# Adding two sums on GpSimd before TensorE turns them, one step later, in a deformable convolution hidden under attention

## The chip, the cores and the metric

One NeuronCore of a Trainium2 chip. The time is the device time of one execution in microseconds (us), the median of the runs shown.

## The reference

A map of 2 images x 128 channels x 48 x 48 passes four residual layers, each `x = x + layer(groupnorm(x))`, in float32: a deformable depthwise convolution, an involution-like layer, a modulated deformable 3x3 convolution and eight-head attention over the 2304 positions of each image. The change concerns the third layer, whose second image is computed while the attention of the first runs:

```python
sampled = bilinear_gather(x, py, px)        # four weighted corners for each of 9 taps
sampled = sampled * mask[:, None]
out = einsum('bckhw,ock->bohw', sampled, w_dc) + b_dc
```

A sample is the sum of four corners, each with its weight. The weights (bilinear times mask) are ready before this stage.

## The kernel before

The attention stage works through 216 windows. In a window TensorE (PE) does eight pairs: `by_query` (L1817), a product whose row maximum VectorE (DVE) takes (L1671), and `score` (L1801), whose exponential ScalarE (ACT) takes (L1547). Scores go through a ring of three PSUM banks, freed by `exp`; `by_query` and everything that DVE takes go through a ring of four banks, freed by DVE. Between pair 2 and pair 3 of a window PE also does `weigh` (L1839), 32 records that add the previous window's exponentials times the values, and, in four of nine windows, `rows` (L1824), which needs the maxima that GpSimd (POOL) has split into three bf16 parts (`split_max`, L1444 to L1447).

Under this runs the gather of the third layer's second image, 18 tiles of 128 positions. A tile has five steps q = 0 to 4 (called beats in the code), one to a window; the first ten steps lie in a lead of 90 maxima ahead of window 0. All four corners of nine taps lie in `corner[:, j % 2]`, two buffers deep, 9 x 512 numbers for each partition.

- POOL starts the indirect DMAs (`fetch`, L1405), three taps (a group) at a time, into the buffer of tile j + 2 while tile j is being turned. A fetch waits until PE has turned that group of tile j.
- ACT multiplies corners 0 and 3 by their weights (`scale_corner`, L1518), 18 short instructions to a tile, at steps 0 to 4 of the tile before.
- POOL multiplies corners 1 and 2 (`weigh_second`, which first waits for the tile's three groups to land, and `weigh_corner`, both L1393), adds corner 2 to corner 1 and, after ACT is done (`add_first`), corner 3 to corner 0 (L1398). So two half-sums are left, in places 0 and 1.
- PE transposes both half-sums of each tap into the same place of PSUM, where the second is added to the first (`turn_samples`, L1887), one group at each of steps 1, 2 and 3; DVE copies a group to SBUF (`take_turned`, L1699). At step 0 of the next tile PE multiplies the nine taps by `w_dc` (`combine`, L1897), and DVE adds the result to x (L1712). At step 1 it takes statistics (L1717).

The class `Entries` writes down the order in which PE fills the banks, so that each engine knows its counts. Work at a step comes after score 5 of the window on PE and after maximum 5 on DVE.

Of the kernel before, what the change touches and what calls it, by code (L numbers as in the profile page):

```python
# [39 lines left out]
TILES = S // 128  # L40
# [4 lines left out]
GROUPS = 3  # L45
GK = K2 // GROUPS
# [69 lines left out]
def semaphores(ctx, nc, prefix, names):  # L116

    return {n: ctx.enter_context(nc.semaphore(f"{prefix}_{n}")) for n in names.split()}
# [421 lines left out]
def middle_layer(nc, g):  # L540

    with ExitStack() as ctx:
# [63 lines left out]
        with nc.Block() as block:  # L606
# [171 lines left out]
            def _(dve):  # L778
# [208 lines left out]
                for step in range(STEPS):  # L987
                    for j in range(K7):
                        if step < ALL_ROWS:
                            multiply(step, j)  # L990
                        beside(step, j)
# [188 lines left out]
class Entries:  # L1180
# [39 lines left out]

    def beside(self, beat):
        j, q = turned_at(beat)
        if 0 <= j < TILES and 1 <= q <= GROUPS:
            self.ab["turned", j, q - 1] = len(self.ab)
        if q == 0 and 1 <= j <= TILES:
            self.ab["combined", j - 1] = len(self.ab)

# [5 lines left out]
def turned_at(beat):  # L1233
    return divmod(beat - FIRST_BEAT, BEATS)
# [12 lines left out]
def attention_layer(nc, g, out):  # L1247
# [6 lines left out]
    with ExitStack() as ctx:  # L1254
        def sb(name, shape, dt=F32):
            return ctx.enter_context(nc.sbuf_tensor(f"l3_{name}", shape, dt))

        s = semaphores(ctx, nc, "l3", ATT_SEMS)
        ps = g["ps"]
# [18 lines left out]
        turned = sb("turned", [128, K2 * 128])  # L1278
        corner, landed = g["corner2"], g["landed2"]
# [34 lines left out]
        def ab_bank(n):  # L1314
            return AB + n % AB_RING
# [12 lines left out]
        with nc.Block() as block:  # L1328
# [59 lines left out]
            def _(pool):  # L1388
                chain = Chain(pool, s["pchain"])
                def weigh_corner(j, c):  # L1390

                    part_c = corner[:, j % 2, :, c * 128:(c + 1) * 128]
                    chain.link(nc.gpsimd.tensor_tensor(  # L1393
                        part_c, part_c, weight[:, j, :, c].unsqueeze(2).to_broadcast([128, K2, 128]), ALU.mult))

                def add_corner(j, c, d):
                    to, by = (corner[:, j % 2, :, i * 128:(i + 1) * 128] for i in (c, d))
                    return nc.gpsimd.tensor_tensor(to, to, by, ALU.add)  # L1398

                def fetch(j, gr):  # L1400
                    if j >= 2:
                        pool.wait_ge(s["ab_full"], no.ab["turned", j - 2, gr] + 1)
                    for k in range(gr * GK, (gr + 1) * GK):
                        at = (TILES + j) * K2 + k
                        nc.gpsimd.indirect_dma_start(  # L1405
                            corner[:, j % 2, k, :], None, g["table2"],
                            bass.IndirectOffsetOnAxis(ap=g["idx2"][:, at:at + 1], axis=0),
                        ).then_inc(landed[j % 2][gr], 16)
# [15 lines left out]
                def weigh_second(j):  # L1424

                    for gr in range(GROUPS):
                        pool.wait_ge(landed[j % 2][gr], 16 * GK * (j // 2 + 1))
                    weigh_corner(j, 1)

                def add_first(j):  # L1430

                    pool.wait_ge(s["scaled"], j + 1)
                    add_corner(j, 0, 3).then_inc(s["mixed"], 1)

                def take_v(n):
                    nc.gpsimd.tensor_copy(v_s[:, n % 2, :, 0:HD], v_all[:, n, :, :]).then_inc(s["v_slot"], 1)
# [20 lines left out]
                def beat(at):  # L1457
                    j, q = turned_at(at)
                    if q == 0 and 0 <= j < TILES:
                        add_first(j)  # L1460
                    if 0 <= j + 1 < TILES:
                        if q == 1:
                            weigh_second(j + 1)
                        if 2 <= q and j + 2 < TILES:
                            fetch(j + 2, q - 2)
                        if q == 3:
                            weigh_corner(j + 1, 2)
                        if q == 4:
                            chain.link(add_corner(j + 1, 1, 2))

                for n in range(LEAD):
                    if n % 9 == 0:
                        beat(n // 9)
                    if n % WPC == WPC - 1:
                        split_max(n // WPC)
# [145 lines left out]
            def _(dve):  # L1621
                chain = Chain(dve, s["gchain"])
# [73 lines left out]
                def take_turned(j, gr):  # L1696
                    at = no.ab["turned", j, gr]
                    dve.wait_ge(s["ab_full"], at + 1)
                    nc.vector.tensor_copy(turned[:, gr * CH:(gr + 1) * CH], ps[:, ab_bank(at), 0:CH]) \  # L1699
                        .then_inc(s["ab_free"], 1)  # L1700
# [7 lines left out]
                def add_sample(j):  # L1708
                    at = no.ab["combined", j]
                    dve.wait_ge(s["ab_full"], at + 1)  # L1710
                    xt = g["x"][:, (TILES + j) * 128:(TILES + j + 1) * 128]
                    nc.vector.scalar_tensor_tensor(xt, ps[:, ab_bank(at), 0:128], g["b_dc"][:, 0:1], xt,  # L1712
                                                   ALU.add, ALU.add).then_inc(s["ab_free"], 1)

                def sample_stats(j):
                    dve.wait_ge(s["ab_free"], no.ab["combined", j] + 1)
                    ins = nc.vector.bn_stats(g["bst"][:, 1, j, :], g["x"][:, (TILES + j) * 128:(TILES + j + 1) * 128])  # L1717
                    if j == TILES - 1:
                        chain.link(ins)

                def beat(at):
                    j, q = turned_at(at)
                    if 0 <= j < TILES and 1 <= q <= GROUPS:
                        take_turned(j, q - 1)
                    if 1 <= j <= TILES:
                        if q == 0:
                            add_sample(j - 1)
                        if q == 1:
                            sample_stats(j - 1)

                for n in range(LEAD):
                    reduce(n)
                    if n % 9 == 8:
                        beat(n // 9)
# [32 lines left out]
            def _(pe):  # L1767
# [6 lines left out]
                for n in range(HALF):  # L1774
                    side, r = 1 - n // NCH, n % NCH
                    if n >= 3:
                        pe.wait_ge(s["part2"], n - 2)
                    nc.tensor.matmul(ps[:, n % 3, 0:CH], g["wqk"][:, side, :], xg[:, r * CH:(r + 1) * CH],
                                     start=True, stop=True).then_inc(s["proj"], 1)
# [7 lines left out]
                def enter_ab(at):  # L1787
                    if at >= AB_RING:
                        pe.wait_ge(s["ab_free"], at - AB_RING + 1)
                    return ab_bank(at)  # L1790
# [90 lines left out]
                def turn_samples(j, gr):  # L1881

                    pe.wait_ge(s["mixed"], j + 1)
                    bank = enter_ab(no.ab["turned", j, gr])
                    for k in range(GK):
                        for c in range(2):
                            last = nc.tensor.matmul(ps[:, bank, k * 128:(k + 1) * 128],  # L1887
                                                    corner[:, j % 2, gr * GK + k, c * 128:(c + 1) * 128], g["ident"][:, :],
                                                    start=(k == 0 and c == 0), stop=(k == GK - 1 and c == 1),
                                                    is_transpose=True)  # L1890
                    last.then_inc(s["ab_full"], 1)

                def combine(j):
                    pe.wait_ge(s["ab_free"], no.ab["turned", j, GROUPS - 1] + 1)
                    bank = enter_ab(no.ab["combined", j])
                    for k in range(K2):
                        last = nc.tensor.matmul(ps[:, bank, 0:128], g["w_dc"][:, k, :], turned[:, k * 128:(k + 1) * 128],  # L1897
                                                start=(k == 0), stop=(k == K2 - 1))
                    last.then_inc(s["ab_full"], 1)

                def beat(at):
                    j, q = turned_at(at)
                    if 0 <= j < TILES and 1 <= q <= GROUPS:
                        turn_samples(j, q - 1)
                    if q == 0 and 1 <= j <= TILES:
                        combine(j - 1)

# [11 lines left out]
                for w in range(WINDOWS):  # L1919
# [3 lines left out]
                    for j in range(PAIRS):  # L1923
# [12 lines left out]
                        if j == BESIDE:  # L1936
                            beat(WARM + w)
                            if w == NORM_AT + 1:
                                bank = enter_ab(no.ab["means"])
# [153 lines left out]
```

## Time and profile before

| | us |
|---|---|
| median of 3 runs | 2173.13 (2167.44 to 2173.97) |
| span of the profiled execution | 2306.6 |
| gather under the attention, windows 1 to about 84 | 1202 to 1696 |
| attention after the gather | to the end |

The profiled execution took 133 us more than the median run. Durations below are its own. A PE record's end is modelled, and matmuls overlap in the array, so the time that a run of matmuls takes is read from one start to the next.

### The profile page before, as it was taken

How to read it: one execution, taken by the hardware profiler on the slowest of the kernel's cores; microseconds unless marked ns; L12 is line 12 of the kernel's file. 1: busy time of each engine (PE TensorE's matmuls, PEld its weight loads, DVE VectorE, ACT ScalarE, POOL GpSimd, SP SyncE). 2: the span in 40 equal slices, each digit the busy share in tenths (PEclk: the TensorE clock that was granted, in tenths of full speed). 3: DMA queues.
4: the chain of work that ended last, by engine and by line, in shares of the span. 5: the costliest groups of instructions: out<-in, count | busy, mean ns of one | idle time of the engine just before them, and what ended most of it. 6: DMA issues, size and time to landing. Idle time of an engine off the chain costs nothing.

```text
span 2306.6 us, 35479 instructions
## 1 busy us (share of the span) xinstructions
PE 1729.9 (75%) x11841; PEld 913.7 (40%) x11841; DVE 1749.1 (76%) x4137; ACT 1186.2 (51%) x3185; POOL 1097.1 (48%) x1232
## 2 busy tenths in 40 slices
PE   4011112116998988786689999999999999999998
PEld 2011111113554456564434444444444444444443
DVE  5477778777999786784587767777788888888881
ACT  3222222210000145556447877787777777777777
POOL 4676777652666355566386766676513000000000
PEclk8555555556999978998779999999999999999999
DMA  8565566540000144446243332333202101020101
GB/s 266 180 186 176 178 184 188 171 135 5 1 1 1 47 135 145 125 151 217 75 124 92 107 90 88 103 104 96 59 10 35 22 19 30 15 34 14 27 1 42
DMA packets 90855, 212.15 MB, mean 92 GB/s; under 512 B 18512, under 2 KB 43824, under 8 KB 90544
## 3 DMA queue, kind: packets, MB, share of 16 engines
q0 software_dynamic: 51840, 169.91, 24.1%
q1 hardware_dynamic: 38832, 39.97, 7.7%
q8 instruction: 94, 1.54, 0.3%
q14 instruction: 89, 0.73, 0.1%
HBM read 175.21 MB, written 13.37 MB: 82 GB/s over the span
## 4 chain that ended last, share of the span: by engine, by line
PE 43%; ACT 3%; DVE 2%; issue 2%; POOL 1%; another core or an unknown queue 0%; SPq 0%; DMA 0%; ACTq 0%; POOLq 0%
PE ps L1801 13%; PE ps L1839 13%; PE ps L1817 11%; ACT l_e L1547 2%; PE ps L1897 2%; DVE l_mx L1671 1%; PE ps L1824 1%; PE ps L1887 1%; ACT corner L1518 1%; PE ps L1851 1%; PE ps L1857 0%; POOL l_part L1414 0%; POOL corner L1405 0%; PE ps L1878 0%
## 5 line engine op out<-in xcount | busy, mean ns | idle before, releaser
L1671 DVE TENSOR_REDUCE l_mx<-ps 128x1 f32<-128x384 f32 x1728 | 837.5, 550 | 162.7 <-PE ps L1817 145.2
L1547 ACT ACTIVATE l_e<-ps 128x384 f32<-128x384 f32 x1728 | 727.0, 511 | 250.0 <-PE ps L1801 236.4
L1817 PE MATMUL ps<-l_ka,l_qs 96*128 96x384 bf16 x1728 | 574.4, 334 | 16.7 <-DMA l_qs<-l_part 8.7
L1801 PE MATMUL ps<-l_qs,l_ks 99*128 99x384 bf16 x1728 | 565.9, 332 | 23.9 <-ACT l_e L1547 18.3
L810 DVE SCALAR_TENSOR_TENSOR m_prod<-ps,c_b,pad 128x384 f32<-128x384 f32 x588 | 325.3, 611 | 77.1 <-PE ps L1015 59.4
L529 PE MATMUL ps<-c_ident,l_samp 128*128 128x128 f32 x324 | 78.5, 427 | 406.2 <-DVE l_samp L392 314.3
L1839 PE MATMUL ps<-l_e,l_v_s 128*32 128x384 f32 x3456 | 336.1, 495 | 2.0 <-ACT l_e L1547 1.0
L1801 PEld LDWEIGHTS ps<-l_qs,l_ks 99*128 99x128 bf16 x1728 | 165.7, 97 | 397.1 <-ACT l_e L1547 216.1
L1444 POOL CAST l_nsp<-l_nm 128x3 bf16<-128x3 f32 x96 | 18.3, 191 | 545.0 <-DVE l_nm L1676 495.2
L250 POOL DMA_INDIRECT corner<-table,idx x216 | 223.1, 1033 | 105.2 <-issue 62.3
L1015 PE MATMUL ps<-red,c_w 32*128 32x384 f32 x1176 | 200.6, 584 | 50.0 <-DVE m_prod L810 40.4
L626 POOL DMA_INDIRECT corner<-table,idx x162 | 170.3, 1051 | 131.2 <-PE ps L1102 60.2
L529 PEld LDWEIGHTS ps<-c_ident,l_samp 128*128 128x128 f32 x324 | 64.2, 224 | 421.8 <-DVE l_samp L392 325.0
L383 DVE SCALAR_TENSOR_TENSOR l_samp<-corner,wts,l_samp 128x128 f32<-128x128 f32 x648 | 185.2, 347 | 53.0 <-remote 30.1
L1817 PEld LDWEIGHTS ps<-l_ka,l_qs 96*128 96x128 bf16 x1728 | 170.1, 98 | 97.6 <-DVE l_mx L1671 32.5
L1405 POOL DMA_INDIRECT corner<-table,idx x162 | 156.3, 965 | 107.2 <-PE ps L1817 42.7
L614 POOL TENSOR_TENSOR m_prod<-m_prod 128x1152 f32<-128x1152 f32 x55 | 144.7, 2631 | 116.5 <-DVE m_prod L810 116.4
L321 ACT ACTIVATE l_samp<-corner,wts 128x128 f32<-128x128 f32 x216 | 70.4, 391 | 203.2 <-DMA corner<-table,idx 158.6
L1839 PEld LDWEIGHTS ps<-l_e,l_v_s 128*32 128x32 f32 x3456 | 111.8, 109 | 104.5 <-issue 71.3
L1030 PE MATMUL ps<-c_ident,m_prod 128*128 128x128 f32 x1008 | 152.9, 301 | 0.3 <-DVE x_map L825 0.3
L1030 PEld LDWEIGHTS ps<-c_ident,m_prod 128*128 128x128 f32 x1008 | 124.5, 155 | 63.4 <-issue 59.0
L383 DVE SCALAR_TENSOR_TENSOR l_samp<-l_corner,wts,l_samp 128x128 f32<-128x128 f32 x324 | 92.5, 348 | 74.4 <-remote 60.1
(212 smaller groups left out, 1961.0 us busy)
## 6 DMA issues: line engine op xcount, KB each, us to landing
corner<-table,idx POOLq DMA_INDIRECT x540
l_ka<-l_part SPq DMA_DIRECT2D x96, 72.0 KB
l_ks<-l_part SPq DMA_DIRECT2D x96, 72.0 KB
table<-l_tok SPq DMA_DIRECT2D x8, 640.0 KB, 6.4
table<-red SPq DMA_DIRECT2D x8, 640.0 KB, 4.9
l_qs<-l_part SPq DMA_DIRECT2D x90, 48.0 KB
l_qs<-l_part SPq DMA_DIRECT2D x96, 24.0 KB
out<-x_map SPq DMA_DIRECT2D x12, 192.0 KB, 1.9
```

The costliest lines, as they stand in the source:

```text
L250: nc.gpsimd.indirect_dma_start(corners[slot][:, k, :], None, from_row[b], bass.IndirectOffsetOnAxis(ap=idx[:, i * K2 + k:i * K2 + k + 1], ...
L383: last = nc.vector.scalar_tensor_tensor(samp[:, slot, k, :], corners[slot][:, k, j * 128:(j + 1) * 128], wts[:, w:w + 1], samp[:, slot, k, ...
L626: nc.gpsimd.indirect_dma_start(corner[:, i % 2, k, :], None, from_row[0], bass.IndirectOffsetOnAxis(ap=idx[:, i * K2 + k:i * K2 + k + 1], ...
L810: nc.vector.scalar_tensor_tensor(prod[:, slot, j, :].rearrange("p (r w) -> p r w", w=W), ps[:, tap % W_RING, 0:CH].rearrange("p (r w) -> p ...
L1015: last = nc.tensor.matmul(ps[:, tap % W_RING, 0:CH], g["w2"][RED * j:RED * (j + 1), ky, half, :], red_of(c)[RED * j:RED * (j + 1), :], sta ...
L1030: last = nc.tensor.matmul(ps[:, ACC, i * 128:(i + 1) * 128], prod[:, row % RING7, j, i * 128:(i + 1) * 128], g["ident"][:, :], start=(ky = ...
L1405: nc.gpsimd.indirect_dma_start(corner[:, j % 2, k, :], None, g["table2"], bass.IndirectOffsetOnAxis(ap=g["idx2"][:, at:at + 1], axis=0),). ...
L1547: nc.scalar.activation(e[:, w % 2, i, :], ps[:, st_bank(at), 0:QC], ACT.Exp).then_inc(s["st_free"], 1)
L1671: nc.vector.tensor_reduce(mx[:, ga % MAX_SLOTS, u // NQC, u % NQC:u % NQC + 1], ps[:, ab_bank(at), 0:CH], AX.X, ALU.max) \
L1801: nc.tensor.matmul(ps[:, bank, 0:QC], ks[:, head % 2, kt * 128:(kt + 1) * 128], qs[:, gb % 3, j * QC:(j + 1) * QC], start=True, stop=True) \
L1817: nc.tensor.matmul(ps[:, bank, 0:CH], qs[0:KROWS, ga // CT % 3, q0:q0 + 128], ka[:, head % 2, k0:k0 + CH], start=True, stop=True).then_inc ...
L1839: last = nc.tensor.matmul(ps[32 * i:32 * i + 32, AV, 0:QC], v_s[:, (gb * CT + i) // NQC % 2, 2 * at + h, :], e[:, w % 2, h * CT + i, :], s ...
```

## The change

POOL adds the two half-sums as well, so one full sum is left in place 0, and PE turns only this one: nine transposes for a tile and not eighteen. PE turns at steps 2, 3 and 4 and not 1, 2 and 3; DVE's copies and the ring's order move with it. POOL's own steps are laid out anew: both multiplications at step 2, the first addition at step 3, two groups fetched at steps 3 and 4, and the third at step 1 of the next tile.

```diff
     def beside(self, beat):
         j, q = turned_at(beat)
-        if 0 <= j < TILES and 1 <= q <= GROUPS:
-            self.ab["turned", j, q - 1] = len(self.ab)
+        if 0 <= j < TILES and 2 <= q:
+            self.ab["turned", j, q - 2] = len(self.ab)
...
                     pool.wait_ge(s["scaled"], j + 1)
-                    add_corner(j, 0, 3).then_inc(s["mixed"], 1)
+                    chain.link(add_corner(j, 0, 3))
+                    add_corner(j, 0, 1).then_inc(s["mixed"], 1)
...
-                        if q == 1:
+                        if q == 1 and j + 1 > 0:
+                            fetch(j + 1, 2)
+                        if q == 2:
                             weigh_second(j + 1)
-                        if 2 <= q and j + 2 < TILES:
-                            fetch(j + 2, q - 2)
+                            weigh_corner(j + 1, 2)
+                        if 3 <= q and j + 2 < TILES:
+                            fetch(j + 2, q - 3)
                         if q == 3:
-                            weigh_corner(j + 1, 2)
-                        if q == 4:
                             chain.link(add_corner(j + 1, 1, 2))
...
-                    if 0 <= j < TILES and 1 <= q <= GROUPS:
-                        take_turned(j, q - 1)
+                    if 0 <= j < TILES and 2 <= q:
+                        take_turned(j, q - 2)
...
                     for k in range(GK):
-                        for c in range(2):
-                            last = nc.tensor.matmul(ps[:, bank, k * 128:(k + 1) * 128],
-                                                    corner[:, j % 2, gr * GK + k, c * 128:(c + 1) * 128], g["ident"][:, :],
-                                                    start=(k == 0 and c == 0), stop=(k == GK - 1 and c == 1),
-                                                    is_transpose=True)
+                        last = nc.tensor.transpose(ps[:, bank, k * 128:(k + 1) * 128],
+                                                   corner[:, j % 2, gr * GK + k, 0:128], g["ident"][:, :])
...
-                    if 0 <= j < TILES and 1 <= q <= GROUPS:
-                        turn_samples(j, q - 1)
+                    if 0 <= j < TILES and 2 <= q:
+                        turn_samples(j, q - 2)
```

## Rows read from the trace of the kernel before

**Rows 1.** The page's first row: the span.

```profile
span 2306.6 us, 35479 instructions
```

**Rows 2.** Busy time by stretch: with the gather, and after it.

```profile
core 0: us, PE busy (x) PEld busy (x) DVE busy (x) ACT busy (x) POOL busy (x), PEclk, DMA share, GB/s
1202.00:1696.00 494.00, 466.33 (x3474) 236.15 (x3466) 371.82 (x822) 374.63 (x1012) 313.24 (x358) 0.98 0.32 89
1820.00:2200.00 380.00, 380.00 (x2864) 157.47 (x2862) 335.04 (x738) 291.11 (x729) 32.06 (x158) 1.00 0.14 24
```

**Rows 3.** TensorE in time, 1636 to 1692: start, length; tiles 16 and 17.

```profile
1636.71 1.50 PE L1839 MATMUL ps<-l_e,l_v_s 128*32 128x384 f32 x16
...
1643.20 0.52 PE L1839 MATMUL ps<-l_e,l_v_s 128*32 128x384 f32 x3
...
1648.43 1.50 PE L1839 MATMUL ps<-l_e,l_v_s 128*32 128x384 f32 x16
...
1650.70 0.82 PE L1887 MATMUL ps<-c_ident,corner 128*128 128x128 f32 x6
1651.36 0.33 PE L1817 MATMUL ps<-l_ka,l_qs 96*128 96x384 bf16 x1
...
1653.65 0.52 PE L1839 MATMUL ps<-l_e,l_v_s 128*32 128x384 f32 x3
...
1658.69 1.50 PE L1839 MATMUL ps<-l_e,l_v_s 128*32 128x384 f32 x16
...
1663.33 0.52 PE L1839 MATMUL ps<-l_e,l_v_s 128*32 128x384 f32 x3
...
1680.41 1.50 PE L1839 MATMUL ps<-l_e,l_v_s 128*32 128x384 f32 x16
...
1685.34 1.50 PE L1839 MATMUL ps<-l_e,l_v_s 128*32 128x384 f32 x16
...
1689.71 0.52 PE L1839 MATMUL ps<-l_e,l_v_s 128*32 128x384 f32 x3
```

**Rows 4.** Groups by line, 1202 to 1696: busy us, mean ns, idle before and releasers.

```profile
L1671 DVE TENSOR_REDUCE l_mx<-ps 128x1 f32<-128x384 f32 x681 | 332.8, 550 | 90.1 <-PE ps L1817 75.7 <-remote 8.1 <-PE ps L1887 5.6
...
L1405 POOL DMA_INDIRECT corner<-table,idx x135 | 129.6, 960 | 74.2 <-PE ps L1817 42.7 <-issue 25.0 <-PE ps L1801 3.7
...
L1398 POOL TENSOR_TENSOR corner<-corner 128x1152 f32<-128x1152 f32 x33 | 86.8, 2631 | 2.6 <-ACT corner L1518 1.6
...
L1887 PE MATMUL ps<-c_ident,corner 128*128 128x128 f32 x306 | 41.8, 272 | 0.0
...
L1444 POOL CAST l_nsp<-l_nm 128x3 bf16<-128x3 f32 x38 | 7.3, 191 | 86.7 <-issue 47.1 <-DVE l_nm L1676 37.0 <-POOL corner L1393 1.4
```

**Rows 5.** The same view, 1820 to 2200, VectorE's maxima.

```profile
L1671 DVE TENSOR_REDUCE l_mx<-ps 128x1 f32<-128x384 f32 x680 | 326.2, 550 | 43.3 <-PE ps L1817 43.3
```

**Rows 6.** All engines in time: two gathers, then ScalarE and VectorE idle.

```profile
1442.44 0.95 POOL L1405 DMA_INDIRECT corner<-table,idx  x1 [0.30 <-issue]
...
1444.26 0.49 ACT L1547 ACTIVATE l_e<-ps 128x384 f32<-128x384 f32 x1 [1.62 <-PE ps L1801]
...
1444.30 1.02 DVE L1671 TENSOR_REDUCE l_mx<-ps 128x1 f32<-128x384 f32 x2 [1.60 <-PE ps L1817]
```

**Rows 7.** TensorE in time around 1355, where six gathers follow one another.

```profile
1354.86 1.50 PE L1839 MATMUL ps<-l_e,l_v_s 128*32 128x384 f32 x16
...
1361.39 0.34 PE L1801 MATMUL ps<-l_qs,l_ks 99*128 99x384 bf16 x1 [3.29 <-ACT l_e L1547]
...
1365.74 2.79 PE L1839 MATMUL ps<-l_e,l_v_s 128*32 128x384 f32 x16
```

**Rows 8.** Busy time by stretch as in rows 2; DMA traffic behind one group.

```profile
1441.00:1443.00 2.00, 2.00 (x22) 0.92 (x22) 1.70 (x4) 1.62 (x5) 1.50 (x2) 1.00 0.50 154
1443.00:1445.00 2.00, 1.80 (x14) 1.23 (x12) 0.70 (x2) 0.74 (x3) 0.39 (x1) 1.00 0.65 225
```

**Rows 9.** TensorE in time, the first transposes of tile 0.

```profile
1177.88 1.54 PE L1887 MATMUL ps<-c_ident,corner 128*128 128x128 f32 x6 [0.78 <-POOL corner L1398]
```

## The prediction

> **What bounds the kernel now.** I began with the span [rows 1] and cut out the two stretches of the attention that matter: with the gather under it, and after it. After the gather PE is busy for all of its 380 us; with the gather it is busy for 466 of 494 us, at a mean granted clock of 0.98, and POOL for 313 [rows 2]. PE's records overlap, so this says "PE or something near it" and no more. The length of a window says what really ends last, and the view for that is PE in time, read from one `weigh` (L1839) to the next, in a place where no gather runs: tiles 16 and 17 [rows 3]. Tile 16 still has ACT's multiplications (of tile 17), all transposes and no fetch. Its steps take 6.49 us (q = 0, with `combine`), 5.23 (q = 1), 5.22 (q = 2), 5.04 (q = 3) and 4.64 (q = 4, no transposes, two multiplications on ACT and not four). Tile 17 has no multiplications: 4.93 for q = 3 with its transposes, 4.37 for q = 4 with neither.
>
> What these tell: two of ACT's multiplications lengthen a window that has no transposes from 4.37 to 4.64, by 0.27. So ACT, which must free the score banks, sets that window and not PE. Six transposes lengthen a window without multiplications from 4.37 to 4.93, by 0.56; so there PE counts nearly in full. With both, 5.04 to 5.23. Several engines are therefore within 0.3 us of each other in each window, and only `combine`'s window is clearly PE's.
>
> A clean tile takes 6.49 + 5.23 + 5.22 + 5.04 + 4.64 = 26.6 us. In the whole stretch 494 us hold 17 combines, 29.1 us a tile. The other 2.4 us come with the fetches and with each batch's turned sums: rows 6 show what a group's third indirect DMA is followed by, ACT and DVE both idle for 1.6 us until signals of PE come, although PE's own records go on. Where six indirect DMAs follow one another and their data is late, a window lasts from 1354.86 to 1365.74 and the next `weigh` needs 2.79 us and not 1.50 [rows 7].
>
> **Removed from PE.** Nine transposes for each of 18 tiles, 162. Their mean duration is 272 ns [rows 4], but they are pipelined: six run from 1650.70 to the next product's start at 1651.36 [rows 3], 0.11 us each. So at most 162 x 0.11 = 17.8 us, if PE ended every window that has them.
> The Trainium skill (TensorE: Matmul & The Clock Gate, section PE-mode transpose) gives some 275 ns for a transpose in a kernel's context, of bf16, which agrees with this duration. Multiplied out it would make 162 x 0.275 = 44.6 us, an estimate that the starts contradict; I take the starts.
>
> **What of this reaches the windows**, step by step, each with its two ends:
> - q = 0: `combine` as before, 6.49. Change 0.
> - q = 1 loses all six transposes and DVE's copy, and keeps four multiplications and the statistics. By the 4.64 of two multiplications plus 0.27 for two more: 4.91, so -0.32. Ends: -0.59 (as 4.64), 0 (if DVE's statistics and maxima hold it).
> - q = 2: three transposes and not six. PE's part falls by 0.33, ACT's bound of 4.91 remains below it, DVE's copy stays: 5.22 to about 5.05, -0.17. Ends -0.33 and 0.
> - q = 3: 5.04 to about 4.95, -0.09. Ends -0.33 and 0.
> - q = 4 had none and gets three, and DVE's copy: PE's plain 4.37 plus 0.33 is 4.70, above ACT's 4.64; I take +0.13. Ends 0 and +0.33 (it adds in full).
> Sum -0.45 us a tile, x 18 = -8.1 us. All gains and no loss would be the -17.8 above; all losses and no gain +6.
>
> **The first tile.** PE waits 0.78 us for POOL's last addition [rows 9]. Its turn is now a step later, past 9 more maxima (over 4 us), while POOL has one addition more (2.63) and three indirect DMAs fewer before it. The wait goes: -1 us with what DVE idles behind it. Ends 0 and -1.2.
>
> **Added to POOL.** One addition of 2.63 us [rows 4], and a wait for the first one's own result, which no row prices; its work is below POOL's slack that follows, and I take nothing for it. POOL's waits in the stretch: 86.7 us before L1444, 74.2 less the 25.0 of fixed issue gaps before L1405 and 2.6 before L1398 [rows 4], together 139, over 17 tiles 8.1 us. The addition leaves 5.4. Then comes a new wait: `weigh_second` now follows directly on the third group's fetch and waits for it to land. A group is 3 x 128 x 2 KB, 786 KB; 308 KB moved from 1441 to 1443 and 450 KB from 1443 to 1445 [rows 8], while the third issue ended at 1443.39 [rows 6]: so it lands some 2 us after the issue. 3.4 us a tile are left, 2.9 after the tile's own gain. Queued behind that wait on POOL are the two multiplications, 4.3 us, and `split_max`, for which PE's `rows` waits, and behind it all scores. `split_max` runs about two windows ahead of `rows` (its batch's maxima are complete by then), 10 us, so a POOL late by 6.5 us does not reach PE. The full sum is needed at q = 2 and begun at q = 0: two windows for 5.3 us. The cover is POOL's remaining 10%; without it, each us that POOL lacks is a us of each tile, 18 in all.
>
> **The moved fetches.** Still 162 indirect DMAs, none more. Group 0 goes from q = 2 to 3, group 1 from 3 to 4, always behind PE's turning of that group; group 2 from q = 4 to 1 of the next tile, where the condition is long met. ACT needs group 0 at q = 0 (before: over two windows after the earliest start, now over one), group 2 at q = 3, two steps after its fetch: with issues 0.95 + 0.30 us apart [rows 6] and 2 us to landing a group takes 5.5 us, one window, so both are met, group 0 with half a window to spare. SP's loads of keys and queries go by their own waits and are not moved past anything. Groups 0 and 1 can no longer follow back to back, since an addition lies between; rows 7 show what a bad pair costs, 5.7 us over a window of 5.2. Whether this, or new coincidences, weighs more I can't read off: 0, ends -12 (two such windows gone) and +6 (one more).
>
> **DVE.** Nothing is added; its copies move from the step with the statistics to the one with little else. Its maxima take 550 ns with the gather and 550 without [rows 4, 5], so POOL's work beside it does not slow it, and one addition more won't either.
>
> **The sum:** -8.1 - 1.0 = -9.1 us. Against the profiled execution: 2306.6 - 9.1 = 2297.5. The runs' median is 2173.1, 133 us less, and I can't place these 133 us; if the pauses of rows 6 belong to them the steps of rows 3, which have none, hold all the more. I take the difference over one to one: 2164.0.
>
> **Rivals.**
> - PE bounds every window (0.13): the whole 17.8 us, and perhaps a bad pair gone; 2155, down to 2148. For it: PE at 100% after the gather. Against it: 4.64 against 4.37 in rows 3.
> - The change does nothing (0.17): DVE and ACT hold q = 1 to 3 and q = 4 takes back what is won; 2170 to 2176. For it: 5.23 and 5.04 differ by less than PE's 0.66.
> - POOL becomes the bound, the other sign (0.15): its tile is 20.9 of work and issue gaps now (29.1 - 8.1), 23.6 with the addition, 25.6 with the landing wait. In the profiled tile of 28.6 that fits; in a clean one of 26.2 it decides once more than 0.6 us of POOL's waits for PE and for maxima can't be used. With 1.5 us a tile is 27.1, 0.5 over today's 26.6, and 18 tiles make 2182; with 2 us 2191. Place: `weigh_second` at q = 2, then PE idle before L1824 or ACT before L1518.
> - The clock (0.03): PE idles more in ACT's windows and its granted clock falls from 2.4 to 1.2 GHz more often than the 0.98 of rows 2 shows; each case costs `weigh` 2.79 - 1.50 and some products, about 3 us; three more make 2173. The skill's same section has it that transposes do not count as busy for the clock; by it taking them away can't lower the clock, which no row here can show.
>
> **How the numbers follow.** My forecast has 0.52, its own range 2157 to 2170. The measurement tells some 0.3%, 6.5 us: faster is below 2166.6. Of my 0.52 about 0.37 lies there, with 0.13 of the first rival 0.50; slower is the third rival and some coincidences of fetches, 0.17; the rest, 0.33, is within 0.3%. The range leaves a tenth on either side: 2152 (between full gain and forecast) to 2181 (POOL short by about 1.5 us a tile).
>
> **What would show it.** L1887 with 162 records; q = 1 windows near 4.9 and q = 4 near 4.8 where no fetch runs; L1398 with 54 records; POOL idle before L1393 some 2 us each tile, waiting for a DMA, and its other waits near half of 139 us; no idle of PE at the first transposes; `combine`'s windows unchanged. Wrong it would be if PE waited before L1824 for POOL, if ACT idled before L1518 for a DMA, or if windows with a fetch grew: a gather's pause now falls in q = 1, which had none.

## The result, and the profile after

The changed kernel takes 2196.49 us (median of 4 runs, 2193.89 to 2198.81) against 2173.55 of the kernel before: ratio 1.0115, 95% interval 1.009 to 1.014. It is slower by 1.2%, where 2164.0 was forecast and 2181 was the upper end.

First, the page: the span, the shares of the chain of work that ended last, and the groups of GpSimd's (POOL's) fetches and of ACT's multiplications (out and in, count, busy us, mean ns of one, idle before and releaser).

```profile
span 2192.7 us, 35162 instructions
...
PE 35%; POOL 9%; ACT 3%; issue 2%; DMA 2%; DVE 1%; SPq 0%; POOLq 0%; ACTq 0%
...
L1405 POOL DMA_INDIRECT corner<-table,idx x162 | 156.3, 965 | 66.4 <-issue 33.8
...
L1520 ACT ACTIVATE corner<-corner,wts 128x128 f32<-128x128 f32 x324 | 131.0, 410 | 38.7 <-DMA corner<-table,idx 38.5
```

Two more groups, from the view by lines of the whole changed kernel, show that the edit did what it should: 54 additions and 162 transposes.

```profile
L1398 POOL TENSOR_TENSOR corner<-corner 128x1152 f32<-128x1152 f32 x54 | 142.1, 2631 | 2.0
...
L1888 PE MATMUL ps<-c_ident,corner 128*128 128x128 f32 x162 | 27.9, 282 | 0.2
```

ACT is idle for 38.5 us until gathered data lands. Lines of this kernel have moved: `score` is L1803, `weigh` L1841, `rows` L1826.

The span is 114 us under that of [rows 1], although the kernel is slower. So the first profile was not of an ordinary execution. A second profile of the kernel before (label b1_before_again) settles it: its span is 2167.4 and its run 2169.3 us. All comparisons below are against this second profile. In it ACT waits once for this gather's data, 4.2 us, and POOL has 1% of the chain that ended last, against 9% in the changed kernel:

```profile
PE 44%; ACT 4%; DVE 2%; issue 2%; POOL 1%; DMA 0%; SPq 0%; ACTq 0%; POOLq 0%
```

Who waited for whom, both kernels, eleven whole tiles of each: us in total, times, longest. PEld is PE's loading of weights. First the kernel before (second profile), 1147 to 1443:

```profile
POOL corner L1405 <- PE ps L1817: 26.5, 21, 3.6
POOL corner L1405 <- issue: 17.8, 60, 0.3
POOL l_nsp L1444 <- issue: 10.4, 3, 5.4
POOL l_nsp L1444 <- DVE l_nm L1676: 8.9, 4, 2.9
```

The changed kernel, 1155 to 1467:

```profile
POOL corner L1393 <- DMA corner<-table,idx: 28.2, 11, 3.5
POOL corner L1405 <- issue: 20.6, 70, 0.3
ACT corner L1520 <- DMA corner<-table,idx: 19.1, 13, 3.8
PEld ps L1826 <- POOL l_nsp L1448: 11.6, 9, 3.1
PE ps L1826 <- POOL l_nsp L1448: 7.5, 4, 2.9
```

Before, POOL waited for PE and for maxima, and neither PE nor ACT for POOL. After, POOL's waits for others are gone. What is left is one wait a tile for a landing, 28.2 / 11 = 2.6 us, and now PE waits for POOL's `split_max` and ACT for data that POOL fetched late. One case in order of time, on POOL and PE of the changed kernel:

```profile
1286.48 4.33 POOL L1393 TENSOR_TENSOR corner<-corner,wts 128x1152 f32<-128x1152 f32 x2 [1.81 <-DMA corner<-table,idx]
...
1293.66 0.95 POOL L1405 DMA_INDIRECT corner<-table,idx  x1 [0.31 <-issue]
...
1294.62 2.62 POOL L1398 TENSOR_TENSOR corner<-corner 128x1152 f32<-128x1152 f32 x1
...
1298.37 0.22 PE L1826 MATMUL ps<-l_identb,l_nsp 128*3 128x128 bf16 x1 [2.87 <-POOL l_nsp L1448]
```

POOL waits for the landing, multiplies, fetches, adds, and only then reaches `split_max`. DVE had finished these maxima at 1288.7, over eight microseconds before `split_max` began; PE stands for 2.87 us before `rows`, and every score is queued behind it. Two other stalls of PE, of 2.1 us (at 1215.0) and 1.9 us (at 1413.2), go by way of ACT: it stands for 3.8 and 2.8 us before a multiplication until fetched data lands, and PE waits for a score bank.

One more thing follows such a wait. TensorE's granted clock (PEclk, the third number from the end) is full before it and half, 1.2 GHz, for a stretch behind it:

```profile
1290.00:1299.00 9.00, 6.13 (x50) 2.88 (x53) 6.19 (x14) 6.05 (x17) 7.67 (x10) 1.00 0.31 89
1299.30:1302.70 3.40, 3.40 (x18) 1.61 (x10) 1.11 (x2) 1.62 (x5) 2.77 (x4) 0.51 0.54 158
```

Between its first `weigh` and its last `combine` the changed kernel has three such stretches of 3.4 us (from 1121.9, 1299.3 and 1490.5), each within a microsecond of PE's return from a wait of 1.6 to 2.9 us for POOL. The second profile of the kernel before has none between these two points.

### The profile page after: what moved, and what is told of

Its sections match the earlier page's. It is cut to its first block, busy times and chain, and to the rows that moved or that the text cites. A ratio compares the mean times of both kernels' runs of the same rounds, so it can differ in the third digit from the quotient of the medians.

```text
span 2192.7 us, 35162 instructions
## 1 busy us (share of the span) xinstructions
PE 1685.3 (77%) x11679; PEld 875.8 (40%) x11679; DVE 1748.9 (80%) x4137; ACT 1188.7 (54%) x3185; POOL 1156.6 (53%) x1250
## 4 chain that ended last, share of the span: by engine, by line
PE 35%; POOL 9%; ACT 3%; issue 2%; DMA 2%; DVE 1%; SPq 0%; POOLq 0%; ACTq 0%
PE ps L1841 11%; PE ps L1803 11%; PE ps L1819 9%; POOL corner L1405 3%; POOL corner L1398 3%; DMA corner<-table,idx 2%; ACT l_e L1549 2%; POOL corner L1393 2%; PE ps L1896 1%; PE ps L1826 1%; DVE l_mx L1673 1%; ACT corner L1520 1%; PE ps L1859 0%; PE ps L1853 0%; POOL l_part L1414 0%
## 5 line engine op out<-in xcount | busy, mean ns | idle before, releaser
L1803 PE MATMUL ps<-l_qs,l_ks 99*128 99x384 bf16 x1728 | 566.2, 332 | 17.4 <-ACT l_e L1549 12.1
L1841 PE MATMUL ps<-l_e,l_v_s 128*32 128x384 f32 x3456 | 336.1, 495 | 2.4 <-issue 1.2
L1803 PEld LDWEIGHTS ps<-l_qs,l_ks 99*128 99x128 bf16 x1728 | 166.0, 97 | 399.1 <-ACT l_e L1549 227.6
L250 POOL DMA_INDIRECT corner<-table,idx x216 | 230.4, 1067 | 92.3 <-issue 65.5
L1015 PE MATMUL ps<-red,c_w 32*128 32x384 f32 x1176 | 194.2, 573 | 38.7 <-DVE m_prod L810 34.3
L626 POOL DMA_INDIRECT corner<-table,idx x162 | 174.7, 1079 | 74.9 <-issue 46.6
L1405 POOL DMA_INDIRECT corner<-table,idx x162 | 156.3, 965 | 66.4 <-issue 33.8
L1841 PEld LDWEIGHTS ps<-l_e,l_v_s 128*32 128x32 f32 x3456 | 112.3, 109 | 104.2 <-issue 74.4
L1520 ACT ACTIVATE corner<-corner,wts 128x128 f32<-128x128 f32 x324 | 131.0, 410 | 38.7 <-DMA corner<-table,idx 38.5
L723 ACT ACTIVATE corner<-corner,wts 128x128 f32<-128x128 f32 x441 | 136.8, 392 | 23.1 <-DMA corner<-table,idx 23.1
L1030 PE MATMUL ps<-c_ident,m_prod 128*128 128x128 f32 x1008 | 147.4, 293 | 1.3 <-DVE m_prod L819 0.9
```

The lines of the kernel that those rows point to most:

```text
L250: nc.gpsimd.indirect_dma_start(corners[slot][:, k, :], None, from_row[b], bass.IndirectOffsetOnAxis(ap=idx[:, i * K2 + k:i * K2 + k + 1], ...
L626: nc.gpsimd.indirect_dma_start(corner[:, i % 2, k, :], None, from_row[0], bass.IndirectOffsetOnAxis(ap=idx[:, i * K2 + k:i * K2 + k + 1], ...
L1015: last = nc.tensor.matmul(ps[:, tap % W_RING, 0:CH], g["w2"][RED * j:RED * (j + 1), ky, half, :], red_of(c)[RED * j:RED * (j + 1), :], sta ...
L1405: nc.gpsimd.indirect_dma_start(corner[:, j % 2, k, :], None, g["table2"], bass.IndirectOffsetOnAxis(ap=g["idx2"][:, at:at + 1], axis=0),). ...
L1520: ins = nc.scalar.activation(at, at, ACT.Copy, scale=weight[:, j, k, c:c + 1])
L1803: nc.tensor.matmul(ps[:, bank, 0:QC], ks[:, head % 2, kt * 128:(kt + 1) * 128], qs[:, gb % 3, j * QC:(j + 1) * QC], start=True, stop=True) \
```

## Where each step's time went

I read each step from one `weigh` to the next, as in [rows 3], for 16 tiles, from the first `combine` in the windows to the last. Medians in us by q, the mean tile, and the time from the first `weigh` to the kernel's end, which leaves out differences of the earlier layers:

| kernel | q=0 | 1 | 2 | 3 | 4 | mean tile | to the end |
|---|---|---|---|---|---|---|---|
| before, second profile | 6.46 | 5.21 | 5.18 | 5.10 | 4.64 | 26.85 | 1067.6 |
| changed | 6.50 | 4.99 | 5.18 | 5.18 | 4.85 | 27.94 | 1088.8 |
| E1, third group at step 0 | 6.46 | 4.99 | 5.18 | 5.11 | 4.72 | 26.79 | 1065.9 |
| E2, new steps, old sums | 6.46 | 4.99 | 5.19 | 5.11 | 4.94 | 27.05 | 1071.2 |
| E3, nine turned, old steps | 6.46 | 5.18 | 5.19 | 5.11 | 4.64 | 26.71 | 1064.8 |
| E8, ACT's multiplications out | 6.21 | 4.68 | 4.72 | 4.77 | 4.72 | 26.07 | 1054.1 |
| E9, as E8, turned twice | 6.21 | 4.54 | 4.94 | 4.99 | 4.94 | 26.14 | 1054.6 |

The changed kernel's medians are nearly those of before. Its mean is 1.1 us higher because in nine of the sixteen tiles one or two windows of steps 3, 4 and 0 last 0.5 to 3.0 us longer than the same windows before, the longest 9.3 us: 16 x 1.09 = 17.4 us, and 4.3 more lie ahead of these tiles, of 21.2 in all. This is what an engine would look like that falls a little behind in each tile: nothing for some windows, then a stall that pays the debt. The three stretches at half clock are part of the stalls; each can have cost at most half of its 3.4 us, so together at most some 5 of the 21 us (an estimate).

## The experiments

**E1: the third group's fetch at step 0**, ahead of the two last additions.

```diff
+                    if q == 0 and 0 <= j < TILES - 1:
+                        fetch(j + 1, 2)
                     if q == 0 and 0 <= j < TILES:
                         add_first(j)
...
-                        if q == 1 and j + 1 > 0:
-                            fetch(j + 1, 2)
```

> The changed kernel, with the third group's fetch at step 0 ahead of the two last additions and not at step 1. Theory A (GpSimd has become the bound, and 2.6 us of each tile are its new wait for the third group to land): that wait lies under 5.3 us of additions, GpSimd's tile falls from 27.9 to about 25.3 us and PE, ACT and DVE set the tile again, near 26.3: 18 x 1.6 = 29 us less than the changed kernel, about 2168, at or a little under the kernel before. Theory B (it is the order on PE and DVE, turning one step later, that costs): nothing changes, about 2196.

Measured: 2173.2 us, ratio to before 1.0011 (0.9997 to 1.0025). Within the noise the whole loss is gone, with one fetch moved by a step. The granted clock is full from the first `weigh` to the last `combine`. POOL's waits in eleven tiles now are again for others, and short:

```profile
POOL l_nsp L1445 <- issue: 6.8, 3, 2.8
POOL corner L1405 <- PE ps L1819: 5.0, 13, 1.4
POOL l_v_s L1437 <- PE ps L1841: 2.8, 4, 1.1
POOL l_nsp L1445 <- DVE l_nm L1678: 2.1, 3, 0.9
```

Theory B falls: E1 turns exactly as late as the changed kernel. It is also no better than the kernel before, so the forecast gain was absent too, not only outweighed.

**E2: the new steps without the new addition.**

```diff
-                    chain.link(add_corner(j, 0, 3))
-                    add_corner(j, 0, 1).then_inc(s["mixed"], 1)
+                    add_corner(j, 0, 3).then_inc(s["mixed"], 1)
...
-                        last = nc.tensor.transpose(ps[:, bank, k * 128:(k + 1) * 128],
-                                                   corner[:, j % 2, gr * GK + k, 0:128], g["ident"][:, :])
+                        for c in range(2):
+                            last = nc.tensor.matmul(ps[:, bank, k * 128:(k + 1) * 128],
+                                                    corner[:, j % 2, gr * GK + k, c * 128:(c + 1) * 128], g["ident"][:, :],
+                                                    start=(k == 0 and c == 0), stop=(k == GK - 1 and c == 1),
+                                                    is_transpose=True)
```

> The changed kernel's steps on all engines, but GpSimd does not add the two half-sums and PE turns both, eighteen transposes to a tile. Theory A: GpSimd's tile is 27.9 - 2.7 = 25.2 us, under what the other engines need, so the time is that of the kernel before, 2170 to 2178; the new wait for the landing is then covered. Theory B (the steps cost): it stays at 2190 or above.

Measured: 2174.56 us, 1.0022 (1.001 to 1.0034). The landing wait is here too, 25.0 us in eleven tiles, and costs next to nothing by itself: POOL still has 2.3 us a tile of other waits.

**E4: each transpose twice**, the second over the first, so that PE has its old amount of work.

```diff
-                        last = nc.tensor.transpose(ps[:, bank, k * 128:(k + 1) * 128],
-                                                   corner[:, j % 2, gr * GK + k, 0:128], g["ident"][:, :])
+                        for _ in range(2):
+                            last = nc.tensor.transpose(ps[:, bank, k * 128:(k + 1) * 128],
+                                                       corner[:, j % 2, gr * GK + k, 0:128], g["ident"][:, :])
```

> The changed kernel, but PE does each of its nine transposes of a tile twice into the same place, so PE has its old amount of work. Theory A: PE has time to spare in the gather, so at most 3 us more, 2196 to 2200. If PE sets the windows: 162 x 0.11 = 17.8 us more, 2214.

Measured: 2195.02 us, 1.0109 (1.0092 to 1.0126), the time of the changed kernel. With POOL as the bound, 162 transposes on PE cost nothing that the runs can tell.

**E3: the removal alone**, in the kernel before; the second half-sum is then missing from the result.

```diff
-                        for c in range(2):
-                            last = nc.tensor.matmul(ps[:, bank, k * 128:(k + 1) * 128],
-                                                    corner[:, j % 2, gr * GK + k, c * 128:(c + 1) * 128], g["ident"][:, :],
-                                                    start=(k == 0 and c == 0), stop=(k == GK - 1 and c == 1),
-                                                    is_transpose=True)
+                        last = nc.tensor.transpose(ps[:, bank, k * 128:(k + 1) * 128],
+                                                   corner[:, j % 2, gr * GK + k, 0:128], g["ident"][:, :])
```

> The kernel before, its steps and GpSimd untouched, but PE turns only the first half-sum, nine transposes to a tile; the second half-sum is left out of the result. It prices the removal alone. By the prediction's steps (q = 1 to 3 shorter by 0.1 to 0.2 us each): 0.45 x 18 = 8 us less, 2164. By the clean profiles since, where steps 2 and 3 took 5.2 and 5.1 us with three transposes as with six: ACT and DVE set these windows and at most 0.1 us a tile is won, 2169 to 2172.

Measured: 2169.74 us, 0.9986 (0.9972 to 1.0000). The tile is 0.14 us shorter, 2.5 us in eighteen, which is at the edge of what the runs can tell. The prediction's term was 8.1.

**E5: the addition alone**, in the kernel before, into a place that nothing reads any more.

```diff
-                    add_corner(j, 0, 3).then_inc(s["mixed"], 1)
+                    chain.link(add_corner(j, 0, 3))
+                    add_corner(j, 2, 1).then_inc(s["mixed"], 1)
```

> The kernel before with one more addition of the same size on GpSimd at step 0, behind corner 3's, into a place that is no longer read. PE turns as before. Theory A: GpSimd's tile is some 20.9 + 2.7 = 23.6 us, there is no wait for a landing behind a fetch, so 0 to 3 us more than before. If the addition itself (its delay of the full sum, or its port beside DVE) cost the 23 us of the change, they are here.

Measured: 2175.25 us, 1.0017 (1.0002 to 1.0031). Together with E2: the addition alone and the landing wait alone cost about 0.2% each; both together cost 1.2%.

**E6: E1 with a fourth addition**, at step 3, behind the third, again into a place that nothing reads.

```diff
                             chain.link(add_corner(j + 1, 1, 2))
+                            chain.link(add_corner(j + 1, 2, 1))
```

> The kernel with the third group at step 0 (2173), with one more addition on GpSimd at step 3, into a place that is no longer read. Theory A is one of a sum, whatever it is made of: GpSimd's tile goes from some 25.3 to 28.0 us, as in the changed kernel, so 18 x (28.0 - 26.8) = 22 us more, about 2195. If it was the particular place of the landing wait that hurt, ahead of the two multiplications, it stays under 2178.

Measured: 2203.86 us, 1.0151 (1.0128 to 1.0174), 9 us more than the expected 2195. There is no landing wait in it, and the stalls are back: the sum decides, not the place. Its tile is 29.2 us (321 for eleven). The half clock may explain the excess: E6 has five such stretches in the gather, 20.5 us in all, which can have cost 10 us at most (an estimate). No run separates this from the added work.

POOL's account, us a tile, over the eleven whole tiles in which it has all its work. Waits are all of POOL's waits but the issue gaps of 0.3 us between indirect DMAs; work is the rest of the tile. Some of these fixed gaps the profile puts down to another engine, and they count as other waits; the changed kernel's 0.3 are nothing else.

| kernel | tile | landing wait | other waits | work |
|---|---|---|---|---|
| before | 26.9 | 0 | 4.6 | 22.3 |
| E5, + addition | 27.0 | 0 | 1.8 | 25.2 |
| E1, + addition, third group at 0 | 26.9 | 0 | 1.8 | 25.1 |
| E2, + landing wait | 27.2 | 2.3 | 2.3 | 22.6 |
| changed, + both | 28.4 | 2.6 | 0.3 | 25.5 |
| E6, E1 + an addition | 29.2 | 0 | 0.8 | 28.4 |

An addition is 2.6 us of engine and 2.9 in the account, 3.3 from E1 to E6. Since work is what is left of the tile, the columns add up by construction; what tells is the column of other waits. It falls from 4.6 us to between 1.8 and 2.3 where one thing is added, and the tile stays at 26.9 to 27.2. Where work and landing wait together (28.1; 28.4 for E6) pass the 26.8 us that the other engines need, hardly any of it is left, and the tile grows.

**E8 and E9: who hides PE's transposes?** E1 with seventeen of ACT's eighteen multiplications left out, so the result lacks these weights; E9 also has E4's edit.

```diff
-                    ins = nc.scalar.activation(at, at, ACT.Copy, scale=weight[:, j, k, c:c + 1])
                     if m == 2 * K2 - 1:
-                        ins.then_inc(s["scaled"], 1)
+                        nc.scalar.activation(at, at, ACT.Copy, scale=weight[:, j, k, c:c + 1]).then_inc(s["scaled"], 1)
```

> The kernel with the third group at step 0 (about 2171), and ACT leaves out seventeen of its eighteen multiplications of a tile; the result lacks these weights. It asks who set the windows of 4.9 to 5.2 us in which PE's fewer transposes bought nothing. If ACT: steps 1, 2 and 3 fall to some 4.7 us, step 4 stays, about 1.1 us a tile, 20 us less, 2151. If DVE: nothing, 2168 or more.

> The same, and PE does each of its nine transposes of a tile twice, its old amount of work. With ACT's cover gone PE's work should count: if ACT alone hid it, 162 x 0.11 = 17.8 us above the run without scaling, 2169. If DVE hides part of it, between 3 and 12 us above it.

Measured: 2162.34 us, 0.9959 (0.994 to 0.9977), and 2162.65, 0.9956 (0.994 to 0.9973). The times alone would say that PE does not matter even here, and both expectations of a time missed: 2151, or 2168 and more, for E8, and at least 3 us above E8 for E9. The steps say otherwise. PE in order of time, E8, steps 1 and 2 of the tile that begins at 1232.69:

```profile
1238.90 0.52 PE L1840 MATMUL ps<-l_e,l_v_s 128*32 128x384 f32 x3
...
1243.44 1.50 PE L1840 MATMUL ps<-l_e,l_v_s 128*32 128x384 f32 x16
...
1248.15 1.50 PE L1840 MATMUL ps<-l_e,l_v_s 128*32 128x384 f32 x16
```

The same in E9, a tile that begins at 1233.34:

```profile
1239.55 0.52 PE L1840 MATMUL ps<-l_e,l_v_s 128*32 128x384 f32 x3
...
1244.10 1.50 PE L1840 MATMUL ps<-l_e,l_v_s 128*32 128x384 f32 x16
...
1249.02 1.50 PE L1840 MATMUL ps<-l_e,l_v_s 128*32 128x384 f32 x16
```

Step 2 is 1248.15 - 1243.44 = 4.71 us in E8 and 1249.02 - 1244.10 = 4.92 us in E9. By the table, without ACT's multiplications steps 2 and 3 fall from 5.18 and 5.11 to 4.72 and 4.77: ACT held them. And now three transposes more cost 0.22 us in each of steps 2 to 4, where they cost nothing in steps 2 and 3 between E1 and E2. That is 0.07 us each, not the 0.11 that the starts gave. The means are level because E8 has tiles of 28.7 and 28.8 us and E9 none. In these two tiles E8's PE waits for POOL before `rows` (1.95 us at 1322.0 and 1.50 at 1426.8) and a stretch of 3.4 us at half clock follows (from 1321.6 and 1427.4). All its waits of this kind, 1154 to 1469:

```profile
PEld ps L1825 <- POOL l_nsp L1448: 7.4, 5, 2.2
PE ps L1825 <- POOL l_nsp L1448: 6.1, 5, 1.9
```

In E9 PE waits so only once, for 0.9 us. POOL's work of 25.1 us (E1's) stands just under the 25.2 to 25.7 us that E8's undisturbed tiles take. So behind ACT the next bound, 0.1 to 0.6 us away, is POOL again.

**E7: `combine` in two.** E1, with five taps at step 0 and four at step 1.

```diff
-        if q == 0 and 1 <= j <= TILES:
-            self.ab["combined", j - 1] = len(self.ab)
+        if q < 2 and 1 <= j <= TILES:
+            self.ab["combined", j - 1, q] = len(self.ab)
...
-                    for k in range(K2):
+                    taps = (range(CUT), range(CUT, K2))[part]
+                    for k in taps:
                         last = nc.tensor.matmul(ps[:, bank, 0:128], g["w_dc"][:, k, :], turned[:, k * 128:(k + 1) * 128],
-                                                start=(k == 0), stop=(k == K2 - 1))
+                                                start=(k == taps[0]), stop=(k == taps[-1]))
...
+                    if part:
+                        dve.wait_ge(s["ab_free"], no.ab["combined", j, 0] + 1)
+                        nc.vector.tensor_tensor(xt, ps[:, ab_bank(at), 0:128], xt, ALU.add).then_inc(s["ab_free"], 1)
```

> The kernel with the third group at step 0, and the product with the nine taps cut in two: five taps at step 0, four at step 1, which has lost its transposes; DVE adds two results to x and not one. Only step 0 is PE's in the clean profiles (6.5 us, other steps 4.7 to 5.2). If that holds, step 0 falls by 4/9 of the 2.0 us to about 5.6 and step 1 grows from 5.1 to about 5.4: 0.6 us a tile, 11 us less, about 2161. If DVE's addition and its own wait for PE take it back, 2170.

Measured: 2164.46 us, 0.996 (0.9945 to 0.9976), 0.4% under the kernel before and better than both kernels. One tile of PE, E7:

```profile
1362.09 1.50 PE L1846 MATMUL ps<-l_e,l_v_s 128*32 128x384 f32 x16
1364.35 1.28 PE L1902 MATMUL ps<-l_turned,c_w_dc 128*128 128x128 f32 x10
...
1367.69 0.52 PE L1846 MATMUL ps<-l_e,l_v_s 128*32 128x384 f32 x3
...
1370.06 1.05 PE L1902 MATMUL ps<-l_turned,c_w_dc 128*128 128x128 f32 x8
...
1373.02 1.50 PE L1846 MATMUL ps<-l_e,l_v_s 128*32 128x384 f32 x16
```

Steps 0 and 1 take 5.60 and 5.33 us, 10.9 against 11.4 in E1. The mean tile is 26.2 us (419.8 for sixteen), 0.55 less than E1's. It uses a step 1 without transposes, which the change gave; whether the same cut would have helped the kernel before was not tried.

**The second profile of the kernel before.**

> The kernel before, profiled once more, since its first profile spans 133 us more than its median run and shows pauses behind each gather that the profile of the changed kernel does not. If these pauses belong to that one execution, this span is near 2172, the sums over the values take 1.5 us in every window of the gather, and a tile takes 26.5 to 27 us. If they belong to the kernel, they are here again.

Measured: one run, 2169.27 us, span 2167.4. A tile takes 26.85 us and not 29.1, and the mean granted clock of 1120 to 1550 is 1.00. The pauses of [rows 6] and the long window of [rows 7] belonged to the first execution. Six gathers in a row stand in the second as well (1241.12 to 1248.40), and the two windows beside them take 5.2 and 5.9 us.

## Why the prediction was wrong

**The step that failed is POOL's account ("Added to POOL").** It took 8.1 us of waits a tile and 20.9 of work, found 3.4 us of slack left behind the addition and the landing wait, and so put nothing for them into the sum. Work is 22.3, and with both it is 28.1 us against the 26.8 that the other engines need. Two errors made up the difference. The 139 us of waits came from 1202 to 1696, and the last two tiles in this stretch have no fetches, the last one no multiplications either; their idle time was shared out over all seventeen. From 1636 to 1696 alone it is:

```profile
POOL l_nsp L1444 <- DVE l_nm L1676: 24.2, 3, 9.8
POOL l_nsp L1444 <- issue: 14.5, 2, 9.3
```

And the tile of 29.1 us in [rows 2] was itself stretched by pauses, in which POOL had rest that it does not have in an ordinary run. Even the first trace, read over its twelve whole tiles alone (1253 to 1603), gives other numbers:

```profile
POOL corner L1405 <- PE ps L1817: 39.0, 23, 4.8
...
POOL l_nsp L1444 <- issue: 18.9, 4, 7.0
POOL l_nsp L1444 <- DVE l_nm L1676: 12.8, 6, 3.6
```

With the smaller waits this is some 6.7 us of 29.2, thus 22.5 of work. With it the prediction's own sum is 22.5 + 2.6 + 2.0 = 27.1, against the 26.2 that it forecast for the new tile and today's 26.6. This is its third rival, with a chance of 0.15, at 2182 us by its own price. The rival's place was right (`weigh_second`, then PE before `rows` and ACT before L1520), as was its condition; its price, 9 to 18 us, was short of the 23 measured. Two of the signs that the prediction named as showing it wrong, PE waiting for POOL before `rows` and ACT idle until a DMA lands, are the ones in the profile.

**The addition itself** was sized right, 2.63 us, and DVE's maxima are no slower beside it: 548 ns after, 550 in [rows 4]. The Trainium skill (GPSIMD Engine Reference, section Elementwise — side-by-side cycle accounting) gives some 2.6 cycles an element for an addition with two inputs on this engine; 1152 elements at its 1.2 GHz are an estimate of 2.5 us, near the row. **The landing wait** was right in kind and near in size, 2 us against 2.6; the addition takes 2.9 in the account.

**"It is covered by two windows"** failed in a way of its own. A lead of ten microseconds covers a delay that comes once. By the account POOL needs 28.1 us in every tile where the others need 26.8, so it falls behind by over 1 us each time. PE first stands for it at 1121.9, ahead of the sixteen tiles of the table, and nine of these have a stall.

**The gain** was too large, and of its sign only E3's 0.14 us a tile is left. Predicted -0.45 us a tile: step 1 -0.32 (measured in E1 -0.22), step 2 -0.17 (0), step 3 -0.09 (0), step 4 +0.13 (+0.08). By means E1's tile has 0.06 less than before. In steps 2 and 3 I let a shorter PE shorten a window that ACT's multiplications set; E8 shows these windows 0.3 to 0.5 shorter when they are gone. The bound for a window that has multiplications and transposes was worked out from windows that had one or the other.

**The rest.** PE's wait of 0.78 us at the first transposes is gone, as predicted, and too small to be seen in the time. `combine`'s window stayed at 6.5, as predicted. The fetches fell together with nothing new where POOL was not the bound (E1, E2). The clock rival, with a chance of 0.03, came true in part and for another reason. It has three stretches at half clock where the kernel before has none, but they follow PE's waits for POOL. E1 and E3, with as few transposes, have none; E4, with the old amount on PE, has two (from 1214.0 and 1295.9). So fewer transposes did not lower the clock in these runs. The `weigh` of 2.79 us in [rows 7] also lies in a stretch at half clock, 1362.9 to 1369.7 of the first profile, behind a wait of PE.

## What to carry to other kernels

Before work is moved to an engine, take its slack from whole periods in which it has all its work, and from an execution whose span agrees with the runs; a mean over a stretch with idle ends, or a stretched trace, shows slack that is not there. Count a new wait as work on an in-order engine, and hold the sum against the period: a lead ahead of the consumer absorbs one delay, not one in each period. And a wait for data just fetched is best put behind work that is there anyway; here one step earlier was worth 23 us.

## What the hardware showed unexpectedly

One execution of the kernel before took 2306.6 us with its profile on, 139 us over the same kernel's second profile. Some 102 of these lie ahead of the first `weigh` (1201.8 against 1099.8) and 37 behind it. In the gather ACT and DVE start up to 0.9 and 0.8 us after the end of the PE product that they wait for; in all eleven other profiles of this study it is never more than 0.3 us. What disturbed the first execution stays open; none of the runs repeats it.

In the gather TensorE's granted clock fell to half, for 3.4 us and once for 6.8, around the end of waits of PE of 1.5 to 3.2 us (the changed kernel, E4, E6, E8), but not behind each of them: the changed kernel waits 1.88 us at 1183.8 and keeps its full clock. So a helper engine that stalls PE can cost more than the wait itself.
